# A gated linear attention block with an RWKV channel mix on one core: how the decay rows and o travel through DRAM, and in which order SyncE moves them

## The reference

```
h = layernorm(x) * (1 + ca) + sa
q, k, v = h Wq', h Wk', h Wv'            # 16 heads of 64
g = -softplus(h Wd' + bd)                # log decay, one per head and token
k = k * sigmoid(h Wg')
s_t = exp(g_t) s_{t-1} + k_t' v_t ;  o_t = q_t s_t
o = o * rsqrt(mean(o*o) + eps) * norm_w * sigmoid(h Wog')
x = x + ga * (o Wo')
h = layernorm(x) * (1 + cb) + sb         # second half: token shift, squared relu
x = x + gb * sigmoid(xr W_r') * (relu(xk W_k')^2 W_v')
```

## Time and profile before

| what | value |
|---|---|
| median of 3 runs | 3420.11 us (3419.12 to 3421.62) |
| the profiled execution, its own time | 3419.12 us |
| its span in the profile | 3416.9 us |
| first load of weights between the passes, issued at | 2076.85 us |
| first load of the second pass, issued at | 2122.17 us |
| mean granted clock of TensorE | 0.991 of full speed |

### The profile page before, as it was taken

How to read it: one execution, slowest core, us unless ns; L and a number is a source line. 1 busy time by engine, 2 the same in 40 slices (tenths; PEclk the granted TensorE clock), 3 DMA queues, 4 the chain that set the end, 5 groups by cost and what they waited for, 6 DMA issues and landing times. The chain is left out here.

```text
span 3416.9 us, 84862 instructions
## 1 busy us (share of the span) xinstructions
PE 3345.7 (98%) x31109; PEld 3070.7 (90%) x31109; DVE 1708.2 (50%) x3988; ACT 1350.5 (40%) x3584; POOL 436.5 (13%) x723
## 2 busy tenths in 40 slices
PE   7999999999999999999999995999999999999998
PEld 6999999999999999999999994898998889899887
DVE  4333333333333333333333335666766776766776
ACT  4444444444444444444444443333333233333322
POOL 0111011011011001110110111211111111111110
PEclk9999999999999999999999997999999999999999
DMA  4322322322322323223223225322223322232330
GB/s 155 109 89 88 105 80 91 105 77 93 105 75 99 100 79 107 85 87 105 80 92 106 71 89 195 93 74 74 81 79 88 84 74 74 74 86 74 92 79 25
DMA packets 233704, 309.17 MB, mean 90 GB/s; under 512 B 16016, under 2 KB 149152, under 8 KB 233648
## 3 DMA queue, kind: packets, MB, share of 16 engines
q1 hardware_dynamic: 233648, 308.40, 29.2%
HBM read 223.40 MB, written 84.93 MB: 90 GB/s over the span
## 5 line engine op out<-in xcount | busy, mean ns | idle before, releaser
L766 DVE SCALAR_TENSOR_TENSOR mid<-state,w_all,psB 128x64 f32<-128x64 f32 x256 | 71.7, 280 | 519.0 <-PE psB L544 519.0
L655 ACT ACTIVATE prob<-cum_rows,w_cur 128x128 f32<-128x128 f32 x1024 | 327.8, 395 | 5.5 <-issue 5.0
L729 DVE SCALAR_TENSOR_TENSOR kg<-gate,psJ 128x256 f32<-128x256 f32 x256 | 107.8, 421 | 408.1 <-PE psJ L57 370.0
L55 PE MATMUL psJ<-h_hi,w_q_hi 128*128 128x256 f32 x1024 | 309.4, 302 | 0.0
L55 PE MATMUL psJ<-h_hi,w_g_hi 128*128 128x256 f32 x1024 | 305.7, 299 | 3.5 <-DVE h_lo L721 3.5
L55 PE MATMUL psG<-h_hi,w_og_hi 128*128 128x256 f32 x1024 | 287.3, 281 | 8.3 <-DMA h_lo<-h_dram 7.4
L55 PE MATMUL psJ<-h_hi,w_k_hi 128*128 128x256 f32 x1024 | 287.1, 280 | 0.7 <-ACT w_new L630 0.7
L56 PE MATMUL psJ<-h_lo,w_g_hi 128*128 128x256 f32 x1024 | 286.5, 280 | 0.0
L57 PE MATMUL psJ<-h_hi,w_g_lo 128*128 128x256 f32 x1024 | 286.0, 279 | 0.0
L56 PE MATMUL psJ<-h_lo,w_q_hi 128*128 128x256 f32 x1024 | 285.9, 279 | 0.0
L57 PE MATMUL psJ<-h_hi,w_q_lo 128*128 128x256 f32 x1024 | 285.6, 279 | 0.0
(11 more groups left out here) (215 smaller groups left out, 9561.1 us busy)
## 6 DMA issues: line engine op xcount, KB each, us to landing
cum_rows<-cum_dram SPq DMA_DIRECT2D x256, 256.0 KB, 3.8
grown<-cum_dram SPq DMA_DIRECT2D x256, 128.0 KB
o_dram<-o SPq DMA_DIRECT2D x256, 128.0 KB, 3.3
o_cols<-o_dram SPq DMA_DIRECT2D x128, 256.0 KB, 5.0
an_norm_x<-in_L_attn_x_dram SPq DMA_DIRECT2D x32, 512.0 KB, 5.4
h_dram<-h_hi SPq DMA_DIRECT2D x32, 512.0 KB, 2.7
h_dram<-h_lo SPq DMA_DIRECT2D x32, 512.0 KB, 4.2
h_hi<-h_dram SPq DMA_DIRECT2D x32, 512.0 KB, 3.8
```

What stands on the lines that cost most here:

```text
L55: nc.tensor.matmul(out, w_hi, x_hi, start=first, stop=False)
L655: last = nc.scalar.activation(prob[:, p % 2, 2 * h + c, :], cum_rows[:, p % 4, 2 * h + c, :], ACT.Exp, bias=w_cur[:, 0, c, 2 * p + h:2 * p ...
L729: nc.vector.scalar_tensor_tensor(out=kg[:, b, :], in0=gate[:, b % 2, :], scalar=1.0, in1=psJ[USES.index(("k", b)) % 2][:, 0:T], op0=ALU.ad ...
L766: nc.vector.scalar_tensor_tensor(out=mid[:, p % 2, :], in0=state[:, p, :], scalar=w_all[:, 0, p:p + 1], in1=psK[:, 0, :], op0=ALU.mult, op ...
```

## The change

It changes the order of the rows in `cum_dram` to kind, chunk, head, and with it the access patterns of `cum_rows` and `grown`; `grown` is loaded by two transfers (one for each head) instead of one. The store of o puts the chunks right, by four transfers of 64 partitions and rows of 512 B, and the second pass loads o by one transfer of the whole tile instead of four. In `sp_tile` the store of o of pair p comes in the turn of pair p, not one later, so its wait is for a copy that ScalarE makes in pair p + 1; `grown` for pair p + 2 is issued behind it; the store of `cum_out` comes ahead of the wait at p = 7 as before, and behind that of o of pair 5. The transpose of the decays comes at the end of pair 6. The small copies of decays become contiguous.

```diff
         def spread_rows(sp, i, p):
             hold(sp, s["e"], NP * i + p - 3)
-            sp.dma_start(cum_rows[:, p % 4, :, :].rearrange("p (h c) t -> p h (c t)", h=2),
-                         cum_b[i, 0, 2 * p:2 * p + 2, :].unsqueeze(0).to_broadcast([P, 2, T])
+            sp.dma_start(cum_rows[:, p % 4, :, :].rearrange("p (c h) t -> p c h t", c=NC),
+                         cum_b[i, 0, :, 2 * p:2 * p + 2, :].unsqueeze(0).to_broadcast([P, NC, 2, CH])
                          ).then_inc(spread[p % 4], 16)
 
         def grow_rows(sp, i, p):
             hold(sp, s["qg"], NP * i + p - 1)
-            sp.dma_start(grown[:, p % 2, :],
-                         cum_b[i, 1, 2 * p:2 * p + 2, :].unsqueeze(1).to_broadcast([2, DH, T])
-                         ).then_inc(grow[p % 2], 16)
-
-        def store_o(sp, j, p):
-            sp.wait_ge(s["o"], NP * j + p + 1)
-            sp.dma_start(o_v[j, :, p, :, :], o[:, p % 2, :, :]).then_inc(store[p % 2], 16)
+            for h in range(2):
+                sp.dma_start(grown[h * DH:(h + 1) * DH, p % 2, :, :],
+                             cum_b[i, 1, :, 2 * p + h, :].unsqueeze(0).to_broadcast([DH, NC, CH])
+                             ).then_inc(grow[p % 2], 16)
...
-                if gla and p + 2 < NP:
-                    grow_rows(sp, j, p + 2)
+                if p == 6 and proj:
+                    sp.wait_ge(s["n_out"], i + 1)
+                    sp.dma_start(cum_v[i], cum_out[:, :]).then_inc(s["n_rows"], 16)
                 if p == 7 and proj:
...
-                if gla and (p > 0 or not opens):
-                    store_o(sp, j if p else j - 1, (p - 1) % NP)
-                if p == 6 and proj:
-                    sp.wait_ge(s["n_out"], i + 1)
-                    sp.dma_start(cum_v[i], cum_out[:, :]).then_inc(s["n_rows"], 16)
+                if gla:
+                    sp.wait_ge(s["o"], NP * j + p + 1)
+                    for h in range(2):
+                        for side in range(2):
+                            sp.dma_start(o_v[j, h * DH:(h + 1) * DH, p, (h + side) % 2, :],
+                                         o[side * DH:(side + 1) * DH, p % 2, h, :]).then_inc(store[p % 2], 16)
+                    if p + 2 < NP:
+                        grow_rows(sp, j, p + 2)
...
-                if k == 0 and turns_decay:
-                    nc.tensor.transpose(psN, w_new[:, 0:2, :].rearrange("p a b -> p (a b)"),
-                                        t["ident"][:, :]).then_inc(s["n_turned"], 1)
...
-                    project(i, "k", p - 1, pe, p == 6)
+                    project(i, "k", p - 1, pe)
...
+                if p == 6 and proj:
+                    nc.tensor.transpose(psN, w_new[:, 0:2, :].rearrange("p a b -> p (a b)"),
+                                        t["ident"][:, :]).then_inc(s["n_turned"], 1)
...
-                load_o(sp, i + 1)
+                sp.dma_start(o[:, :, :], o_v[i + 1]).then_inc(s["ol"], 16)
...
-    cum_b = cum_dram.rearrange("i (a h c) t -> i a h (c t)", a=2, c=NC)
+    cum_b = cum_dram.rearrange("i (a c h) t -> i a c h t", a=2, c=NC)
```

More of the change, by code:

```diff
@@ L341, in attention_pass @@
         qg = sb("qg", [P, 2, T])
-        grown = sb("grown", [P, 2, T])
+        grown = sb("grown", [P, 2, NC, CH])
         gate = sb("gate", [P, 2, T])
@@ L397, in grow_rows, with sp_tile @@
             hold(sp, s["qg"], NP * i + p - 1)
-            sp.dma_start(grown[:, p % 2, :],
-                         cum_b[i, 1, 2 * p:2 * p + 2, :].unsqueeze(1).to_broadcast([2, DH, T])
-                         ).then_inc(grow[p % 2], 16)
-        def store_o(sp, j, p):
-            sp.wait_ge(s["o"], NP * j + p + 1)
-            sp.dma_start(o_v[j, :, p, :, :], o[:, p % 2, :, :]).then_inc(store[p % 2], 16)
-        def sp_tile(sp, i, gla, proj, prep, opens=False):
+            for h in range(2):
+                sp.dma_start(grown[h * DH:(h + 1) * DH, p % 2, :, :],
+                             cum_b[i, 1, :, 2 * p + h, :].unsqueeze(0).to_broadcast([DH, NC, CH])
+                             ).then_inc(grow[p % 2], 16)
+        def sp_tile(sp, i, gla, proj, prep):
             j = i - 1
@@ L436, in _ @@
             sp_tile(sp, 0, False, True, 2)
-            sp_tile(sp, 1, True, True, 2, True)
+            sp_tile(sp, 1, True, True, 2)
             with sp.Fori(2, NT - 2) as i:
@@ L442, in _, with project @@
             sp_tile(sp, NT, True, False, 0)
-            store_o(sp, NT - 1, NP - 1)
             for n in range(2):
-                sp.wait_ge(store[n], 16 * NP // 2 * NT)
+                sp.wait_ge(store[n], 64 * NP // 2 * NT)
             sp.wait_ge(s["h_kept"], 32 * NT)
-        def project(i, kind, b, pe, turns_decay=False):
+        def project(i, kind, b, pe):
             u = USES.index((kind, b))
@@ L640, in copy_o @@
             act.wait_ge(s["gla"], n + 1)
-            hold(act, store[p % 2], 16 * (NP // 2 * j + p // 2))
+            hold(act, store[p % 2], 64 * (NP // 2 * j + p // 2))
             nc.scalar.copy(o[:, p % 2, :, :], psO[:, :, :]).then_inc(s["o"], 1)
@@ L654, in act_tile @@
                         for h in range(2):
-                            last = nc.scalar.activation(prob[:, p % 2, 2 * h + c, :], cum_rows[:, p % 4, 2 * h + c, :], ACT.Exp,
+                            last = nc.scalar.activation(prob[:, p % 2, 2 * h + c, :], cum_rows[:, p % 4, 2 * c + h, :], ACT.Exp,
                                                         bias=w_cur[:, 0, c, 2 * p + h:2 * p + h + 1], scale=-1.0)
@@ L735, in grow_q @@
             dve.wait_ge(s["by_act"], act_done(j, ("q", p)))
-            dve.wait_ge(grow[p % 2], 16 * (NP // 2 * j + p // 2 + 1))
+            dve.wait_ge(grow[p % 2], 32 * (NP // 2 * j + p // 2 + 1))
             hold(dve, s["gla"], n - 1)
-            nc.vector.tensor_tensor(qg[:, p % 2, :], q[:, p, :], grown[:, p % 2, :],
+            nc.vector.tensor_tensor(qg[:, p % 2, :], q[:, p, :], grown[:, p % 2, :, :].rearrange("p c t -> p (c t)"),
                                     ALU.mult).then_inc(s["qg"], 1)
@@ L781, in dve_tile @@
                     dve.wait_ge(s["soft"], i + 1)
-                    nc.vector.tensor_scalar(g_raw[:, :].rearrange("p (h c) -> p c h", c=NC), zt[:, 0, :, :], -1.0, None,
+                    nc.vector.tensor_scalar(g_raw[:, :], zt[:, 0, :, :].rearrange("p c h -> p (c h)"), -1.0, None,
                                             ALU.mult).then_inc(s["g_raw"], 1)
@@ L802, in dve_tile @@
                     nc.vector.tensor_copy(w_all[r, :, :],
-                                          w_new[r, 3, :].rearrange("p (b h c) -> p h c b", c=NC, h=2)[:, h, :, :])
-                nc.vector.tensor_copy(w_cur[:, :, :, :], w_new[:, 0:3, :].rearrange("p a (h c) -> p a c h", c=NC)).then_inc(s["cur"], 1)
+                                          w_new[r, 3, :].rearrange("p (c b h) -> p h c b", c=NC, h=2)[:, h, :, :])
+                nc.vector.tensor_copy(w_cur[:, :, :, :].rearrange("p a c h -> p (a c h)"),
+                                      w_new[:, 0:3, :].rearrange("p a b -> p (a b)")).then_inc(s["cur"], 1)
                 gate_k(dve, i, NP - 1)
@@ L908, in load_h @@
                 sp.dma_start(h[:, :, :].bitcast(F32), h_v[i, :, part, :, :]).then_inc(s["hl"], 16)
[L910 to L915, removed]
         def sp_tile(sp, i, att, ffn, prep):
@@ L935, in _ @@
             load_h(sp, 0)
-            load_o(sp, 0)
+            sp.dma_start(o[:, :, :], o_v[0]).then_inc(s["ol"], 16)
             sp_tile(sp, 0, True, False, True)
@@ L1039, in act_tile @@
             if att:
-                act.wait_ge(s["ol"], 64 * (i + 1))
+                act.wait_ge(s["ol"], 16 * (i + 1))
                 hold(act, s["ss"], i)
@@ L1281, in adaln_gla_block @@
             prepare(nc, t, jobs, "s")
-            output_pass(nc, t, W, x_v, o_v, h_v, out_v)
+            output_pass(nc, t, W, x_v, o_dram, h_v, out_v)
 _INS = ["L0_attn_x", "L0_attn_Wq", "L0_attn_Wk", "L0_attn_Wv", "L0_attn_Wo", "L0_attn_Wg", "L0_attn_Wog", "L0_attn_Wd",
```

## The result

The changed kernel takes 3543.72 us (median of 4 runs, 3541.36 to 3552.08) against 3420.70 of the kernel before beside it: a ratio of 1.0365, 95% interval 1.0347 to 1.0382. It is slower by 123 us. The forecast was 3446 with a range up to 3480, so the direction was right and the size far off. The profiled execution took 3546.25 us with its span of 3544.1, 127.2 more than the span before.

The account below looks back on a forecast made before the run. The prediction took TensorE to bound the kernel, with losses showing only beyond their cover or in the tail. Steady stall 17.7, tail 9.8 and second pass -1.0 made +26.5 on 3419.1, so 3445.6 us, range 3421 to 3480.

Parts of the forecast that it names:

- The bound and the place: TensorE busy 3345.7 of 3416.9 us; losses show only in the tail or once their cover is used up.
- step 1: SyncE's issues: 7 a pair instead of 3, about 5.2 us, under the pair's 6.2, so no bound in steady tiles.
- step 2: Steady tiles: `grown` behind o's wait and four stores; pair 3 stalls 0.61 us beyond 1.75 of cover, 17.7 us over 29 tiles.
- its term of 2.1 us: Time from the issue of the second half of `grown` to its landing, taken as 2.1 us, ends 1.9 and 3.0.
- zero: Moving the transpose of the decays to the end of pair 6 was to cost nothing.
- (b): Rival: landing of `grown` nearer 3.0 us, lower TensorE clock possible in the tail; +55 us, 3475; chance 0.15.
- step 3: Last tile: the chain from o's copy to `mid` 2.65 us longer, three times, plus a later last store: +9.8 us.
- step 4: Second pass: one 1 MB load of o instead of four removes the wait for the sigmoid at its start: -1.0 us.
- (a): Rival: only the tail shows, no steady stall; 3428 us, or 3424 with cheap stores; chance 0.27.
- (c): Rival: not slower, only the second pass's 1.0 us left, 3418 us; chance 0.08 with unforeseen gains.

Follow-up runs that it names:

- run 4: The changed kernel with the decay rows as before (1 and 2 KB), `grown` still in two loads: 3465.16 us, ratio 1.0130.
- run 8: The kernel before with only the transpose of the decays moved to the end of pair 6: 3427.46 us, ratio 1.0020.
- run 9: The kernel before with the transpose of the decays later inside the same projection (`k == 2` for `k == 0`): 3427.82 us, ratio 1.0022.
- run 7: The changed kernel with the load of x behind `grown` of pair 3 and the stores of h in the turn of pair 4: 3493.85 us, ratio 1.0211.
- Run 11: The changed kernel with `grown` issued ahead of the wait for o in the last tile alone: 3524.33 us, then 3523.09 (ratio 1.0293).
- run 14: The kernel before with two stores of o a pair that put the chunks right, and one load of o in the second pass: 3419.14 us, ratio 0.9997.
- run 13: The changed kernel measured again as it is, on one chip with two variants: 3532.98 us, ratio 1.0327 to the kernel before.
- run 10: The kernel before with all new transfers and layouts, its SyncE order kept and the transpose back inside the projection: 3425.94 us, ratio 1.0016.
- run 2: The kernel before with the new order on SyncE alone, one store of o and one load of `grown` a pair: 3473.20 us, ratio 1.0156.
- run 3: The changed kernel with one store of o a pair instead of four, and four loads of o in the second pass: 3443.28 us, ratio 1.0069.
- run 1: The changed kernel with `grown` of pair p+2 issued ahead of the wait for o of pair p: 3438.29 us, ratio 1.0052.
- run 5: All transfers and layouts of the changed kernel, its transpose at the end of pair 6, in the SyncE order of before: 3431.54 us, ratio 1.0033.
- run 6: The changed kernel with one store of o a pair and 1 KB decay rows, `grown` in two loads, late order kept: 3433.65 us, ratio 1.0043.

## Why the prediction was wrong

**The bound and the place: right.** TensorE was full, the loss came through `grown`, `qg`, `mid` and `prob` at the transposes, and in the tail.

**SyncE's queue (step 1, and the times of issue in step 2): right, in part by luck.** Shifted by the copy of o for pair 0 (1047.29 to 1032.71, so -14.58), the forecast has stores of pair 0 at 1033.25 (measured 1033.25), h at 1037.77 (1037.73), `cum_rows` at 1039.68 (1039.70), the stores of pair 1 at 1040.90 (1040.98) and `grown` of pair 3 at 1043.94 (1043.78). A store issues in 494 ns (median) and four in 2.4 to 2.6 us, where 0.58 and 3.04 were taken; a load of `grown` in 671 ns for 565. The times fit because these two errors nearly cancel.

**The landing of `grown` (step 2, its term of 2.1 us): the step that failed.** "I take 2.1, with 1.9 and 3.0 as ends." From the first issue of a pair's two to the start of `qg` the forecast had 0.74 + 2.1 = 2.84 us. Measured in pair 3: 1048.91 - 1043.78 = 5.13; in pair 2, 1040.37 - 1035.92 = 4.45. The row that the estimate was built on, `cum_rows` with 256 KB in 3.0 us, is of pieces of 2 KB; the new loads are pieces of 512 B, and scaling by bytes (3.0 less 1.12 x 3/4) was wrong in kind: the median is 3.4 (run 4: 2.6 with pieces of 1 KB), and for pair 3 it is 4.1. `qg` of pair 3 came 2.13 us later than forecast on a cover of 1.75 that the forecast had already used up. That is why an error of 2 us showed nearly in full: the stall is 2.09 instead of 0.61 in pair 3 and 0.32 instead of 0 in pair 2, together 2.41 where 0.61 + 2.13 = 2.74 would be all of it. So the waits are 67.8 us instead of 17.7, and with what they bring (the clock, below) the steady part is 106.9 longer. The upper end, 3.0, was no bound of the cost; it was a row of another form.

**The transpose (step 2, "zero"): wrong by 7 us**, shown by runs 8 and 9, by a matmul spacing that no row of before was read for.

**The clock in the steady part: not thought of.** Rival (b) has it for the tail alone. It is some 15 us here, and it comes and goes with the stall: with 0.9 us of it a tile (26 us idle in run 7) the clock stays. Of the +39.1 us of busy time the clock explains 15 and the transpose 7; about 17 are not attributed. An estimate for part of them: TensorE stops 70 times in the steady part, 3 times before, and the last matmul ahead of a stop counts with its whole 0.28 us, where the next one otherwise starts 0.11 us behind it; 67 x 0.17 is 11 us.

**The tail (step 3): +9.8 forecast, +17.1 and 2.7 for the last stores measured.** The link from the end of a copy of o to the `mid` two pairs on was forecast at 5.44 us and measured at 2167.99 - 2160.64 = 7.35: stores 2.38 (2.36 forecast), then 4.89 from the first load's issue to `mid`, where 0.56 + 2.1 + 0.42 = 3.08 were taken. It is the same landing, taken too short, and two issues of 1.66 us together for 1.12. The passes through the link are three, as forecast. The granted clock is 0.50 from 2168 on, as rival (b) said; how much of the 17 is that was not separated. Run 11 takes 10 us off the tail and with them a part of both: the mean granted clock of the tail in its first profile is 0.83, for 0.75 in the changed kernel and 1.00 before.

**The second pass (step 4): -1.0 forecast, -2.2 measured.** The wait for `og` is gone as forecast; the further 1.2 come with the one load of o too (run 14 has -2.4 with nothing else changed in that pass), by what way is not explained.

**The rivals.** (a) fell: the steady part lost 107 us. (c) fell. (b) named the cause, and its 3475 was still 69 us short: the landing was beyond its 3.0 and the drops of the clock in the steady part weren't in it.

**Parts that don't add.** Over the kernel before, the order alone costs 53 us, the transfers alone 11, both together 123 (113 in run 13). Taking away the order gives back 105, the stores 100, the small rows 79 (some 10 less each, if held against run 13). One chain with a fixed cover is enough to explain this: copy of o, stores, issue, landing, `qg`, `mid`, `prob`. Each part lengthens it, and only what goes beyond the cover is paid, then in full in 29 tiles. Below it nothing is: run 10's steady part is that of before. TensorE's idle time in the steady part goes the same way: 68.7 us in the changed kernel, 30.7 in run 2, 26.4 in run 7, 16.0 in run 4, 3.5 in run 3, 1.6 in run 1 and 0.9 in runs 5, 6 and 10.

## What to carry to other kernels

Where a load is moved behind a wait, add up the whole chain to the instruction that the bound engine needs and compare it with the cover; when the sum comes within a microsecond of the cover, the forecast is a coin toss over the whole loss, and the range must say so. Price the landing of a transfer by a row with the same size of piece and the same number of pieces, not by its bytes. And issue loads that depend on nothing late ahead of waits that do: here it is two lines, worth 95 to 105 us.

## What was not expected of the hardware

- **The landing of these loads goes with the number of pieces.** 128 pieces of 512 B: 3.4 us; 64 of 1 KB: 2.6. The load of `cum_rows`, 256 KB, in the changed kernel 256 pieces of 1 KB: 5.6, and 3.8 as 128 pieces of 2 KB, 3.7 in run 4. At 128 pieces, four times the bytes add 0.4 us. The stores don't show it: 64 pieces of 512 B land after 1.9 us, and so do 128 of 1 KB in run 6. Page of the changed kernel (KB of one, us to landing):

```profile
cum_rows<-cum_dram SPq DMA_DIRECT2D x256, 256.0 KB, 5.6
grown<-cum_dram SPq DMA_DIRECT2D x512, 64.0 KB, 3.4
o_dram<-o SPq DMA_DIRECT2D x1024, 32.0 KB, 1.9
```

- **The price of an issue goes with its form**: 494 ns for a store of 64 rows of 512 B (but 542 for that of `cum_out`, of the same shape, in the same profile), 671 for a load of 64 times 2 rows of 512 B, 516 for 64 rows of 1 KB, 0.37 us for a store of 128 rows.
- **The spacing of matmuls** of one form is 0.113 or 0.118 us, and where a single transpose stands some projections earlier decides which: 0.2 us in a tile of 63.
- **The clock after short idleness**: it stood at half for 3.4 us in 8 to 11 tiles of 31 (four profiles, those of runs 11 and 13 among them), behind or around waits of 1.9 to 3.0 us in the changed kernel. In 18 other tiles there, with longest waits of 1.2 to 2.6 us, it didn't fall, nor in the kernel before, nor in runs 2 and 7, whose tiles wait some 1.0 and 0.9 us in all.
